# A hand-merged program of attention, state space filter and mixture of experts: the order tables are replaced

## The reference

```
xn = layernorm(x)
Q, K = xn @ Wq, ctx @ Wk                       # 4 heads of 32
s = Q K^T / sqrt(32)                           # per head 512 x 1024
p = softmax over the 32 largest of each row, 0 elsewhere
c = mean over heads(p) @ (ctx @ Wv)            # 512 x 256
u = layernorm(xn) * (1 + m * scale_in(c)) + m * shift_in(c)
y = s4d(u)                                     # long convolution, by Fourier transform
y = y * (1 + m * scale_out(c)) + m * shift_out(c)
t = xn + y;  t = t + gelu(layernorm(t) @ W1 + b1) @ W2 + b2
x = x + tanh(g0) * layernorm(t)
h = layernorm(x);  logits = h @ gate_w;  e = argmax;  sc = sigmoid(max)
routed = swiglu_e(h * sc)                      # one of 8 experts a token
x = x + tanh(g1) * (swiglu_shared(h) + routed)
```

## Time and profile before

| what | value |
|---|---|
| median of 3 runs | 1769.05 us (1768.24 to 1775.35) |
| the profiled execution's own time | 1771.37 us |
| its span | 1768.8 us |
| busy, PE / DVE / ACT / POOL | 1415.4 / 1340.8 / 1149.1 / 1196.7 us |
| mean granted clock of PE | 0.859 |
| frame 0 (68.6 to 248.1) | 179.5 us, DVE busy 159.54, clock 0.65 |
| frame 3 (590.5 to 761.3) | 170.8 us, DVE busy 151.34, clock 0.84 |
| frame 6 (1128.6 to 1307.4) | 178.8 us, DVE busy 153.89, clock 0.90 |
| frame 7 (1307.4 to 1485.0) | 177.6 us, DVE busy 153.81, clock 0.89 |
| after the last attention tile | 1485 to 1768.8 |

### The profile page before, as it was taken

The page is one execution under the profiler, slowest core; times in us unless marked ns, Lnnn a source line. Parts: engine busy times, 40 slices in busy tenths (PEclk is TensorE's granted clock), DMA queues, the critical chain, the costliest instruction groups (busy, mean ns, idle before and its releaser), DMA issues.

```text
span 1768.8 us, 20269 instructions
## 1 busy us (share of the span) xinstructions
PE 1415.4 (80%) x6251; PEld 1001.3 (57%) x6251; DVE 1340.8 (76%) x2168; ACT 1149.1 (65%) x2101; POOL 1196.7 (68%) x1341
## 2 busy tenths in 40 slices
...
DMA packets 97214, 115.12 MB, mean 65 GB/s; under 512 B 17840, under 2 KB 74168, under 8 KB 96964
## 3 DMA queue, kind: packets, MB, share of 16 engines
...
## 4 chain that ended last, share of the span: by engine, by line
PE 42%; DVE 19%; ACT 15%; POOL 14%; issue 6%; DMA 3%; SPq 1%; POOLq 0%; DVEq 0%; ACTq 0%
DVE R L1440 7%; DVE ZB L1444 5%; PE PS L2012 4%; PE PS L2126 4%; POOL ZB L753 3%; PE PS L1787 3%; PE PS L1975 3%; PE PS L2080 3%; PE PS L1986 3%; ACT R L1032 3%; DVE ZB L1436 3%; POOL ZB L755 3%; ACT ZB L1029 2%; PE PS L2099 2%; ACT R L1035 2%
## 5 line engine op out<-in xcount | busy, mean ns | idle before, releaser
L1440 DVE MAX8 R<-ZB 128x8 f32<-128x1024 f32 x384 | 469.8, 1225 | 9.3
L1444 DVE MATCH_REPLACE8 ZB<-R,ZB 128x1024 f32<-128x1024 f32 x256 | 309.3, 1208 | 0.0
L753 POOL TENSOR_TENSOR ZB<-ZB 128x1024 f32<-128x1024 f32 x96 | 234.2, 2440 | 70.6 <-ACT ZB L1029 70.3
L1032 ACT ACTIVATE R<-PS 128x512 f32<-128x512 f32 (+6 forms) x404 | 176.3, 468 | 157.3 <-PE PS L1986 28.3
L755 POOL TENSOR_TENSOR ZB<-ZB 128x1024 f32<-128x1024 f32 x96 | 226.6, 2360 | 7.5
L1432 DVE MAX8 R<-PS 128x8 f32<-128x1024 f32 x128 | 156.0, 1219 | 23.2 <-PE PS L1762 23.2
L1436 DVE MATCH_REPLACE8 ZB<-R,PS 128x1024 f32<-128x1024 f32 x128 | 155.4, 1214 | 0.3 <-issue 0.3
L2072 PE MATMUL PS<-R 128*128 128x512 f32 x256 | 138.4, 687 | 14.5 <-ACT R L1336 13.3
L1029 ACT ACTIVATE ZB<-ZB,R 128x1024 f32<-128x1024 f32 x128 | 147.1, 1149 | 4.2
L1761 PE MATMUL PS<-ZR 97*128 97x512 f32 x128 | 83.9, 656 | 80.8 <-ACT ZB L1071 65.7
L751 POOL TENSOR_TENSOR ZB<-ZB 128x1024 f32<-128x1024 f32 x32 | 75.5, 2359 | 102.9 <-ACT ZB L1029 102.1
...
## 6 DMA issues: line engine op xcount, KB each, us to landing
...
R<-xs_d SPq DMA_DIRECT2D x39, 128.5 KB, 2.1
...
```

The costliest lines, as they stand in the source:

```text
L753: pool.tensor_tensor(e, e, w, ALU.mult).then_inc(s.g_att, 1)
L1032: return act.activation(o, i, ACT.Copy, **k)
L1440: vec.max(ml[:, 8 * r:8 * r + 8], w).then_inc(s_tk[n % 2], 1)
L1444: vec.match_replace(w, ml[:, 8 * r:8 * r + 8], w, NEG).then_inc(s_tk[n % 2], 1)
```

## The change

Every table of slots gets new numbers; no line outside the tables changes, and no instruction is added or removed. The new numbers come from a replay of the program that also models the half clock of an idle TensorE. What matters of them is the order that results. Of 4261 steps, 363 stand elsewhere against their neighbours: 44 of 1257 on ACT, 132 of 1360 on DVE, 46 of 542 on POOL, 124 of 889 on PE and 17 of 213 on SP. Apart from one step of POOL (weights, 45 places later) none moves by more than 9 places. The moves that the prediction speaks of:

- Setup, PE: weight 0, ray 1 (L1879), weight 1, ray 2, in place of ray 1, ray 2, weight 0, weight 1. Weight 2 (L1861) stands ahead of the first reduction product (L1902), not behind it.
- Frame 0, SP: the late loads (L592, L593) go out two kernel-row writes (L625) later. PE: score 0.13 ahead of the context steps (L1802, L1807), not behind.
- Start of frame, PE: av, shdown 0 to 3, score .2 in place of av, shdown 0 and 1, score .2, shdown 2 and 3. ACT copies all four before EXP .1.
- DVE: tile .2's last maximum ahead of tile .3's first; tile .4 up to max 2, then the four spectrum steps, the rest of .4, and only then .5 (before, .4 and .5 alternated); max 0 of tile .8 after replace 2 of tile .7.
- ACT: norm 0 somewhat earlier against its neighbours.
- SP, frames 4 to 6: the input of the next sample (L577), the residual's x (L638), then tile 2, 6 or 10. Before, L638 stood early in the frame. PE: score .8 between the gate and the up matmuls (L2099) of that tile, not ahead of them.
- After the last attention tile, POOL: scatter (L993) of tile 16 ahead of the spectrum steps, of tiles 17 and 18 after the four b2 steps (L873). Before: 16 and 17 between the spectrum and the inverse steps, 18 after the first b2 step. SP: L638 of sample 7 and its stores ahead of tile 20's down weights.

The diff, cut to the tables that make these moves:

```diff
-ACT_SH = ((151.2, -80.2, 151.6, -52.6), (143.6, 112.4, -230, -340.5))
+ACT_SH = ((149.7, 117.9, 24, -47.9), (141.9, 142.4, -93.5, -33))
...
-ACT_NORM = ((66.1, 124.8), (-574.9, 50.3))
+ACT_NORM = ((68.3, 130.6), (-593.6, -347.3))
...
-ACT_EXP = (18.9, 15.4, 16.9, -342.7, 6.1, 6.3, 6.5, 10.5, -136, 19.7, 6.4, 20.5, 22.3, -13.2, 18.3, 21.8)
+ACT_EXP = (20, 14, 22.8, -322.1, 17.9, 14.3, 13, 19.1, -1.8, 25, -66.4, 21.2, 20, -37, 23.9, 23.2)
...
-DVE_SPECTRUM = ((109.8, -120.1, 111.8, -381.3), (54.3, -166.3, -118.6, -647.3))
+DVE_SPECTRUM = ((119.6, -294.1, 10.5, -56.4), (54.5, -115.1, 37.4, -210))
...
-PE_SCORES = (-17.8, -8.4, -13.1, -16.3, -20.3, -26.2, -27.3, -29.2, -28.9, -28.4, -29.4, -29.2, -33.4, -34.6, -37.2, -26.9)
+PE_SCORES = (-17.3, -8.8, -13.9, -16.3, -19.1, -24.3, -25.7, -28.5, -31.2, -26.6, -28.9, -31.3, -33.5, -36.7, -29.5, -30.6)
...
-SP_POST = ((137.8, 140, -477.2, 85.8, -161.6), (98.3, 137, -121.1, -296, -247.4))
+SP_POST = ((138, 138.9, -684.4, -162.4, -596.8), (84, 87.9, -37.8, -447.2, -563.4))
...
-SP_INPUT = (82.9, 136.9)
+SP_INPUT = (81.7, 136.2)
...
-SP_LATE = (137.2, 250.9)
+SP_LATE = (137.3, 262.1)
...
-SP_CHUNK = (134.8, 139.4, 137.7, 137.5, 122.2, 253.3, 254.1, 261.7, -2979.7)
+SP_CHUNK = (137.3, 135.3, 137.7, 122, 136.3, 250.3, 252.6, 262.9, -4223.2)
...
-PE_WEIGHT = (-51.7, -51.2, -35, -24, 1, 1.1)
+PE_WEIGHT = (-60.3, -52.3, -40.3, -24.5, 0.3, 1.5)
...
-PE_RAY = (-80, -62.5, -54.5)
+PE_RAY = (-80, -55.3, -47.8)
...
-ACT_WEIGHT = (-130.1, 10, -1357.9, 15.6, 14)
+ACT_WEIGHT = (-24.5, 4.6, -2046.4, -36.3, 21.2)
...
-ACT_RAY = (-23.2, -11.1, 2.2)
+ACT_RAY = (-15.9, -6.8, 2.6)
...
-POOL_WEIGHT = (96.6,)
+POOL_WEIGHT = (145.4,)
...
-POOL_SPECTRUM = ((122.6, -404, 85.9, 13.8), (72.9, -141.4, -790.5, -646.9))
+POOL_SPECTRUM = ((122.2, -889.9, -21.2, 36.2), (127.9, -90.2, -957.7, 127))
...
-POOL_INV = ((126.7, -427.9), (127, 121.3))
+POOL_INV = ((125, -236.2), (106.1, 102.3))
...
-POOL_TILE = ((125.2,), (127.3,), (130.7,), (132.5,), (250.6,), (-194,), (128.3,), (148.2,), (-1221.3,))
+POOL_TILE = ((123,), (127.3,), (129.6,), (132.4,), (251.2,), (135.7,), (56.4,), (146.2,), (-885.5,))
...
-POST_AT = ((5.6, 7.6, 8, 8.7, 13.5, 14.2, 16.6, 17.2, 18.6, 18.6, 23, 24.2, 24.4, 24.8, 43.1, 43.5, 45.6, 46.2, 48.8, 50.3,
-          52.1, 53, 55, 55.7, 58.1, 60.9, 62.4, 62.6, 97.2, 99, 102, 104.7, 104.8, 103.3, 105.4, 107.6, 109.9, 110.1, 123.1,
-          126.1, 127.5, 128.5, 128.5, 131.7, 132.9), (5.8, 9.6, 10.7, 11.2, 14.2, 14.7, 18.4, 19.1, 21.8, 22.2, 23.6, 31.5,
+POST_AT = ((3.3, 3.4, 4.3, 6.7, 15.1, 15.3, 16.1, 16.7, 18.5, 19.2, 26.5, 26.6, 26.6, 26.7, 43.7, 44.7, 45.6, 46.3, 48.5,
+          49.7, 51.2, 51.7, 54.9, 55, 55.6, 57.4, 62, 63.2, 93.1, 95.1, 95.5, 101.9, 102.9, 98.3, 104.6, 105.6, 106.7, 111.9,
+          113.1, 114.8, 116.8, 128.4, 128.9, 129.2, 129.5), (1.7, 2.4, 2.8, 3.5, 5.8, 6.6, 7.6, 9.3, 14.4, 16.6, 16.8, 16.9,
...
-DVE_TOP = ((42.9, 43.6, -109.5, 44.9, -215.1, 49.5, -188.5), (43.1, -377.9, -133.4, -26.1, 44.9, 59.2, -46.5), (54.9, 67.4,
-          -123.5, 5.3, 45.3, -85.8, 71.1), (60.2, 51.4, 45.7, -29, 73.6, 79.4, -532.8), (72.6, 74.9, 77.7, -323.7, 79.2, 80.8,
-          -603.3), (67.8, 75.5, 78.7, 3.2, -133.5, -280.9, -233.8), (71.3, 73.3, -4.3, -139.6, -148.1, -84.6, -57.6), (67.5,
+DVE_TOP = ((49.7, 14.4, 9.8, 50.5, -396.3, 51.1, -269.1), (45.1, -414.7, 22, -123.3, 65.7, -160, -441.7), (62, 85.2, -120.4,
+          74.1, 76.8, -429, -292.8), (87.1, -142.6, -228.3, -72.3, -88, 91.7, -712.9), (86.1, 27.2, -22.1, -501, 36.7, 95.3,
+          -1079), (92.1, -107.6, 94.8, -25.6, -101.4, -405.3, -717.1), (87.1, 95.1, -52.2, -42.8, 82.8, -338.7, 32.7), (88.2,
...
-SP_TILE = ((137.4, -133.4, 70.4), (-1217.7, 120.1, 133.4), (139.3, 58, -39), (130.2, -23.1, 139.8), (-189.8, 31.4, -3.9), (12,
-          -43.8, -952.7), (42.7, -47.6, -106.9), (107.1, 101.2, -369.3), (-293.5, 105.9, 94.8))
+SP_TILE = ((137, 136.6, 85.5), (-1816, 106.4, 117.9), (138.3, 14.9, -236.8), (129.9, 27.4, 138.8), (-24.3, 2.4, 139.4),
+          (-12.1, -133.8, -1123.9), (21.1, -520.4, -196.8), (52.8, -5.2, -196.3), (-533.8, 76.5, 111.4))
...
```

More of the change, by code:

```diff
@@ new lines @@
+POOL_INV = ((125, -236.2), (106.1, 102.3))
+POOL_FILM_OUT = ((101, -622.3, -810.7, -1159.5), (52.1, -198.8, -216.6, -756.9))
+POOL_ROOT = ((127.8, 131.8, 132.3), (-118.9, 140, -1))
+POOL_RESIDUAL = ((130.2, 93.5, -205.5, 128.2), (-537.4, 81.3, 71.1, 17.4))
+POOL_OUT = ((-3233.4, -266.8, -964.8, -1435.2), (-1425.4, 6.7, -33.8, 24))
+POOL_ROUTE = ((132.5, 111.4, -338.3), (119.3, -541.6, -437.5))
+POOL_SH = ((237.9, -775.4, -26.5, 161.9), (148.8, 109.4, -836.7, -2653.6))
+POOL_PREP = (72.6, 73.7)
@@ new lines @@
+POOL_LOW = (109.7, 74.4, 76.4)
+ACT_FILM_IN = ((27.5, 18.4, -514.6, -13.7), (15.7, -604.1, 29.3, -460.9))
+ACT_INV = ((51.7, -3.9), (72.3, -349.8))
+ACT_FILM_OUT = ((56.1, -98.9, -518.4, -708.3),)
+ACT_ROOT = ((66.8, 113.6, 127.4), (79.5, -3553, 112.1))
+ACT_NORM = ((68.3, 130.6), (-593.6, -347.3))
+ACT_TURN = ((77.6, -237.6), (88.3, -520.6))
+ACT_UP = ((90.6, -176.1, -76.2, -314.7, 76, -377.8, 98.3, -364.5), (95.1, 60.6, -1334.7, -224.8, -990.1, 37.5, 64.9, -755))
+ACT_DOWN = ((106.2, 47.2, -246.4, 111.1), (-5.7, -17.5, 0.3, 104.2))
@@ new lines @@
+ACT_OUT = ((115.7, -641.3, -333.4, 41.7), (25, -974.6, -1463.3, -1274.7))
+ACT_TURN2 = ((133.8, -2159.2), (136.9, -1027.2))
+ACT_ROUTE = ((-4011.8, 86.5), (-1710.3, 127.6))
+ACT_SILU = ((131.4, 144.8), (-41.5, -53.9))
+ACT_SH = ((149.7, 117.9, 24, -47.9), (141.9, 142.4, -93.5, -33))
+DVE_SPECTRUM = ((119.6, -294.1, 10.5, -56.4), (54.5, -115.1, 37.4, -210))
+DVE_MOMENTS = ((146.9, 168.6), (-367.7, 106.8))
+DVE_ROUTE = ((172.7, 174.2), (117.6, 35.6))
+ACT_PREP = (15.4, 22.9, -1435)
+ACT_QUERY = (34.8, -151.9, 43)
@@ new lines @@
+ACT_CONTEXT = (17, 59.4)
+ACT_KEY = (27.7, 62.1)
+ACT_FINISH = ((11.7, -721.2, 13, 21.1), (23.1, -294.7, 30.1, 42), (18.1, -61.6, 30.5, 43.4), (0.6, -13.2, 15, 18.7))
+POOL_SUM = (109.2, 107.8, 105.2, 42.8, 92.5, 86.6, 80.6, 73.6, 65.9, 59.3, 51.7, -21.5, 36.3, 28.4, 21, -4)
+ACT_EXP = (20, 14, 22.8, -322.1, 17.9, 14.3, 13, 19.1, -1.8, 25, -66.4, 21.2, 20, -37, 23.9, 23.2)
+ACT_SUM = (-5819.9, -3399.7, -14141.3, -1289.2, -2392.4, -2831.2, -4431.8, -1749.9, -625.5, -1768.8, -1088.2, -1898.5,
+          -9504.6, -2913, -3279.4, -4181.4)
@@ new lines @@
+ACT_MOMENTS = (9.8, 12)
+PE_WEIGHT = (-60.3, -52.3, -40.3, -24.5, 0.3, 1.5)
+ACT_WEIGHT = (-24.5, 4.6, -2046.4, -36.3, 21.2)
+DVE_WEIGHT = (-21.1,)
+POOL_WEIGHT = (145.4,)
+DVE_RAY = (-59.8, -607.6, 18.6)
+ACT_RAY = (-15.9, -6.8, 2.6)
+PE_RAY = (-80, -55.3, -47.8)
+DVE_CHUNK = ((6.4, -112), (49.7, 81.6), (104.3, 111.2), (132.7, 137), (144, 148.2), (152.7, 147), (158.2, 162.3), (160.5,
+          166.1))
+PE_CHUNK = ((-43.7, -35.7, -19.2, -1, 1.5, 7), (0.1, 1, 6.4, 7.3, 14.1, 14.3), (8.1, 9.1, 9.4, 14.7, 19.9, 23.8), (16.3, 19.4,
+          26.4, 27, 35.4, 42.1), (28.1, 28.6, 31.5, 33.4, 48.4, 48.9), (40.4, 43.8, 44.1, 47, 60.2, 60.8), (50.3, 53.5, 60.5,
+          60.8, 64.6, 64.6), (60.9, 61.4, 61.4, 66.7, 83.7, 92.5))
@@ new lines @@
+ACT_CHUNK = ((-551.5, -1800.5), (16.1, 32.1), (24.2, 44.8), (52.5, 60), (64.7, 69.9), (78.6, 84.3), (94.3, 105), (105.1,
+          115.3))
+ACT_VALUE = ((8.2, 24.9, -6770.2), (-507.9, 42.5, -16059.7), (-1011.7, 56.5, -17175.8), (-573, 78.3, -15512.8), (-2117.9,
+          87.2, -16634.1), (-2186.1, 105, -12043.4), (-850.1, 114.4, -9488), (-2122.8, 125.2, -14674.2))
+POOL_CHUNK = ((94.8, -351.5, 80.3, -1349.3), (-743.4, -696, 117.8, -1847.2), (-387.5, 20.4, 123.5, -527.1), (-376.2, -496.8,
+          127, -2542), (-293.2, -141, 129.5, -2395.9), (31.2, -771.4, 129.9, 10.6), (-169.8, -131, 131.5, -1286.9), (-225,
+          -88.9, 132, -1229.2))
```

96 lines of the change are left out of this document (26 added, 70 removed), and 12 rows, old and new, of tables (DVE_TOP, POST_AT).

## The result

| | before | after |
|---|---|---|
| median beside each other | 1770.66 us (4 runs) | 1748.13 us (1746.67 to 1752.08, 4 runs) |
| ratio | 1 | 0.9873, 95% interval 0.9845 to 0.9902 |
| profiled execution / its span | 1771.37 / 1768.8 us | 1746.72 / 1744.7 us |
| mean granted clock | 0.859 | 0.882 |

The new order is 22 us faster (17 to 27 by the interval), where 6 were forecast. Direction and range held; the size did not, and the prediction's own last sign of being wrong came true: frames 1 to 7, from the first maximum of tile 1.0 to that of the last tile, became 12.7 us shorter, and it allowed 10. Ratios of an experiment stand against the kernel before, run on the same chip; a difference of two ratios is turned into time by 1770 us, and is uncertain by some 6 us.

A forecast was written before the change was run, and what follows sets the result against it. No engine was full and the chain of waits was shared, with DVE's maximum passes pacing frames 1 to 7; -6 -5 +6.3 -7 +9 -3 = -5.7 us from 1769.05 gave 1763 us, range 1742 to 1783.

The forecast's parts named there:

- (a): Setup: weight steps ahead of ray steps let PE start the angles earlier and shorten DVE's waits, -6 us.
- (b): Frame 0: late loads two kernel-row writes later, score ahead of context steps, removing a wait of about 7 us, -5 us.
- (c): Start of frames 1 to 3: undivided shared down step ahead of score .2 delays POOL's sum for DVE, +6.3 us.
- (d): DVE's order inside a frame: un-mixed passes cost 0.9 us, earlier spectrum shortens later waits; -1 a frame, -7 us.
- (e): Frames 4 to 6: extra load ahead of tile weights and score .8 between gate and up, 3 a frame, +9 us.
- (f): After the last attention tile: POOL's scatters reordered, so the film steps come earlier, -3 us.
- rival A: The frames gain: DVE's two long waits of the spectrum step fall by over half in seven frames, 1735 to 1749 us; chance 0.28.
- Rival D: Frame 0: joined PE idle times keep its clock high, about -4 us, giving 1759 us; chance 0.06.

The follow-up runs named there:

- e12: The kernel before with SyncE's late loads (gs and W2, 2 MB) alone moved two kernel-row writes later: 1765.23 us, ratio 0.9968.
- e2: The kernel before with value matmuls behind score .15 and DVE's share of block 2 behind the second replace of tile .14, samples 1 to 6: 1772.83 us, ratio 1.000.
- e8: The kernel before with the new order of all engines from tile 7.14 on: 1769.77 us, ratio 0.9987.
- e9: The kernel before with six unused matmuls added ahead of the turn before the gate, at the end of frames 1 to 3: 1771.17 us, ratio 1.0006.
- e7: The changed kernel with DVE's whole old order: 1790.09 us, ratio 1.008 against the kernel before.
- e1: The changed kernel with the value matmuls moved back ahead of score .15 on PE, samples 1 to 6: 1764.2 us, ratio 0.9962 against the kernel before.
- e5: The changed kernel with the residual's x issued ahead of the next sample's input again, frames 1 to 6: 1754.13 us, ratio 0.9895 against the kernel before.
- e4: The changed kernel with SyncE's whole old order: 1762.37 us, ratio 0.9929 against the kernel before.

## Why the prediction was right in direction and short in size

(a) Right but for the size: 4.6 of 6. The PE side came out to 0.1 us; the miss is that I let DVE keep its old time for its last ray step, which now waits 4.61 us for weight step 0 and ends 4.3 us later.

(b) Right: -5.1 by the trace, -5.7 by e12. Not foreseen were the 4.2 us that the first nine tiles of frame 0 lose; 2.0 of them are a new wait of DVE for value matmuls and 1.1 more work of DVE in the stretch. They need not be the new order's: in the traces of e2, e8 and e12, which have the old order there, the same stretch is 3.0 to 3.1 us longer than in that of before.

(c) Too high. Counted from the first maximum of its frame, POOL's pass of the earlier trace rows starts 0.8 us earlier in frame 1, 1.8 later in frame 2 and 1.0 earlier in frame 3, not 2.1 later in each, and from .0 to .9 frames 1 to 3 lose 1.9 us together, not 6.3. I took the chain as rigid from ACT's copies to DVE. The wait of DVE for that sum became shorter, not longer, 15.8 to 5.4 us over the program. With DVE's old order it is long (17.1 to 20.2 in e2, e8, e9 and e12, and 13.6 in e7, where nothing else of after is undone) and with the new one short (2.9 to 6.6 in the others), so DVE's new order takes this wait away; I had priced the un-mixing as a loss of 0.9 us a frame.

(d) This is the step that failed. Its term, -1 a frame for an earlier spectrum, left out what stood in the same tables: the value matmuls behind score .15 and the share behind a replace. The swap itself has no term: it fell under my sentence that most moves exchange work on an engine that has both ready, and cost nothing, and the stretch from tile .14 to .15 stood at 0. It has a price through the clock of what follows: in frame 3 2.4 us on turn and gate (6.30 to 3.85 from the start of the one to the end of the other), and another 1.5 on shared matmuls and rank (DVE's wait of 1.94 became 0.41). Frames 1 to 7 gained 17.6 us there, and e1 gives back 13.3 of them in its trace and 16 us of the whole time. DVE's long wait for L751, which (d) named, hardly moved in frame 3 (4.4 to 4.1), and the other, for the gate, fell from 3.7 to 1.3, by the clock and not by an earlier chain. My sign for (d), both waits below 8 us together, was met (5.4), but not for my reason.

(e) Wrong by nearly its whole 9 us. The waits grew as I worked out (4.47 to 5.12, 1.20 to 2.05), but the second half of the up matmuls took 2.39 us at a granted clock of 0.81 (3.17 before; the first half took 3.79 at 0.50), and counted from the tile's first matmul (L2089) the up step ended 0.6, 0.0 and 0.1 us later in tiles 2, 6 and 10. So the burst did not stay at the low clock to its end, as I had let it. e5 bounds the rest: the extra load costs nothing that can be measured, and frames 4 to 6, without their steps from .14 to .15, together became 1.6 us longer, not 9.

(f) BATCH_NORM came 3.05 us nearer to DVE's last film step (L1614), as worked out. By the turn (L2001) 1.0 was left of it, and another 1.9 came by the down steps behind. A further 2.7 us, which I had not foreseen, were gained between the last tile's first maximum and that film step. e8 gives 2.3 +-3.8 us for the end as a whole.

That the 7 us left without the swap (e1) are close to my 6 is in part luck: the +4.2 in frame 0 had no term, and of the +8.3 forecast for (c), (d) and (e) together +2.9 came. The range held because its lower end lay 21 us below the forecast, on the strength of rival A and not of the swap. Rival A had the size (its upper end was 1749) with the wrong cause. Rival D had the cause with the wrong place: I gave it frame 0, where the clock from 50 to 100 us is 0.70 in after too, the same as in the earlier trace rows, and 6% of chance. I should have asked of each pair of PE steps that change places how long PE stands idle ahead of the first burst that DVE waits for.

What stays open. That the swap brings its 16 us by the clock is read from the traces; no run gives the order without the clock, and e9, the clock without the order, gains nothing that can be told from zero. Frames 2, 4 and 6 of after have a step of 19.3 to 19.5 us, with the clock falling in the gate or behind it, in the same order in which frames 1 and 3 have 15.7; what tips it wasn't found. Nor was L1464 itself changed (off POOL's passes, or to a form with one operand in SBUF), which would show whether the step can be had at 15.7 each time. By the steps of 15.7 and 16.7 in e4 that is some 3 us in each of the three frames.
